# Attention score products on two row tiles of TensorE, one plain with one shifted head at a time

## What is computed

```
def _mha(q_in, k_in, v_in, Wq, Wk, Wv, bv, causal):
    q, k, v = projections of q_in, k_in, v_in to 16 heads of 16 values
    scores = einsum('bhse,bhte->bhst', q, k) * 16 ** -0.5
    if causal: scores = where(tril, scores, -inf)
    return softmax(scores) @ v, heads side by side
sa = _mha(x, x, x, ..., causal=True);   x = _layernorm(sa + x)
ca = _mha(x, ctx, ctx, ..., causal=False);   x = _layernorm(x + ca)
ffn = relu(x @ Wf1 + bf1) @ Wf2 + bf2;  x = _layernorm(x + ffn)
```

## Time and profile before

| | us |
|---|---|
| median of 3 runs (lowest, highest) | 1575.48 (1568.61, 1591.3) |
| the profiled execution, whole / its span | 1561.23 / 1559.5 |
| mean granted TensorE clock in it | 0.854 of 2.4 GHz |
| PE busy in the span | 1208.1 (77%) |
| DVE / ACT / POOL busy | 988.3 / 614.3 / 456.5 |
| PE plain products L403 (512) | 98.5 busy |
| PE shifted products L425 (512) | 76.6 busy |
| ACT exponentials L510 (128) | 117.2 busy |

### The profile page before, as it was taken

The page is one execution under the profiler, slowest core; times in us unless marked ns, Lnnn a source line. Parts: engine busy times, 40 slices in busy tenths (PEclk is TensorE's granted clock), DMA queues, the critical chain, the costliest instruction groups (busy, mean ns, idle before and its releaser), DMA issues. The chain is left out here.

```text
span 1559.5 us, 25872 instructions
## 1 busy us (share of the span) xinstructions
PE 1208.1 (77%) x9362; PEld 803.9 (52%) x9362; DVE 988.3 (63%) x2640; ACT 614.3 (39%) x1214; POOL 456.5 (29%) x609
## 2 busy tenths in 40 slices
PE   2898889999499710788888888830599996799998
PEld 1475555555278610577767677730254553345554
DVE  6646776676247530788888888845465651477776
ACT  1435556565255200566656665510054543000000
POOL 2325663323426644123333333245110100100000
PEclk9768998998689855799999999975586875699999
DMA  6313233221023234566566655335221211101000
GB/s 203 79 46 90 79 78 111 62 69 35 21 83 116 93 120 170 203 233 232 197 220 229 233 200 210 108 105 190 66 60 45 79 33 36 40 28 35 28 7 14
DMA packets 122052, 167.14 MB, mean 107 GB/s; under 512 B 13747, under 2 KB 96454, under 8 KB 118982
## 3 DMA queue, kind: packets, MB, share of 16 engines
q1 hardware_dynamic: 115894, 154.45, 30.1%
q0 software_dynamic: 3584, 8.92, 1.8%
q10 hardware_dynamic: 2448, 2.13, 0.4%
HBM read 123.31 MB, written 41.94 MB: 106 GB/s over the span
## 5 line engine op out<-in xcount | busy, mean ns | idle before, releaser
L1944 PE MATMUL moe_ps_u<-moe_x_hl,moe_up_hl 128*128 128x256 f16 x1932 | 226.8, 276 | 70.5 <-DVE moe_up_hl L2020 43.9
L1944 PEld LDWEIGHTS moe_ps_u<-moe_x_hl,moe_up_hl 128*128 128x128 f16 x1932 | 184.6, 99 | 112.7 <-DVE moe_up_hl L2020 50.4
L2307 PE MATMUL mix_ps_e<-wr_hl,mix_u_hl 128*128 128x512 f16 x768 | 173.4, 382 | 0.0
L2020 DVE SCALAR_TENSOR_TENSOR moe_up_hl<-moe_up_in,moe_up_hl 128x512 f16<-128x512 f32 x161 | 123.3, 798 | 55.5 <-ACT moe_up_hl L1993 55.5
L2064 POOL CAST moe_mid_hl<-moe_mid 128x256 f16<-128x256 f32 x161 | 71.7, 445 | 293.7 <-DVE moe_mid L2035 293.7
L2419 DVE SCALAR_TENSOR_TENSOR mix_acc<-mix_ps_e,mix_shares,mix_acc 128x256 f32<-128x256 f32 x256 | 110.3, 476 | 40.0 <-PE mix_ps_e L2307 39.7
L510 ACT ACTIVATE dec_probs<-dec_ps_t 128x768 f32<-128x768 f32 (+1 forms) x128 | 117.2, 917 | 38.5 <-PE dec_ps_t L425 38.1
L1993 ACT ACTIVATE moe_up_hl<-moe_up_in 128x512 f16<-128x512 f32 x161 | 99.2, 619 | 63.1 <-DMA moe_up_in<-in_moe_w 63.1
L1266 DVE TENSOR_REDUCE memory_neg_m<-memory_ps_s 128x2 f32<-128x512 f32 x128 | 84.8, 689 | 61.2 <-PE memory_ps_s L1043 58.6
L2307 PEld LDWEIGHTS mix_ps_e<-wr_hl,mix_u_hl 128*128 128x128 f16 x768 | 75.1, 98 | 84.0 <-issue 2.2
L403 PE MATMUL dec_ps_s<-dec_k_st,dec_q_st 48*128 48x256 f16 (+1 forms) x512 | 98.5, 277 | 20.3 <-DVE dec_neg_m L618 10.8
(11 more groups left out here) (278 smaller groups left out, 2098.0 us busy)
## 6 DMA issues: line engine op xcount, KB each, us to landing
moe_up_in<-in_moe_w SPq DMA_DIRECT2D x23, 1792.0 KB, 7.5
moe_down_in<-in_moe_w SPq DMA_DIRECT2D x23, 896.0 KB, 4.6
moe_raw<-in_mix_wr SPq DMA_DIRECT2D x32, 256.0 KB, 7.7
dec_q_st<-dec_q_dram SPq DMA_DIRECT2D x96, 64.0 KB, 2.7
dec_k_st<-dec_k_dram SPq DMA_DIRECT2D x96, 64.0 KB, 2.8
xs<-zeros SPq DMA_DIRECT2D x8, 736.0 KB
moe_x_in<-xs SPq DMA_DIRECT2D x23, 256.0 KB, 4.3
ys<-moe_y SPq DMA_DIRECT2D x23, 256.0 KB, 7.6
```

The costliest lines, as they stand in the source:

```text
L1944: mm = nc.tensor.matmul(bank[:, m, :], up_hl[t.slot][:, w, m, dc, f * P:(f + 1) * P], x_hl[t.slot][:, x, dc, :], start=(dc == 0 and w == x ...
L2020: nc.vector.scalar_tensor_tensor(up_hl[t.slot][:, LO, :, :, at].rearrange("p m c h -> p (m c) h"), up_in[t.slot][:, :, :, at].rearrange("p ...
L2307: mm = nc.tensor.matmul(ps_e[fill % RING][:, :, :], u_hl[t.slot][:, r, dc, k * P:(k + 1) * P], wr_hl[:, m, dc, 2 * q:2 * q + 2, :], start= ...
```

## The change

Even heads' stacks go to partitions 0-48 of `q_st` and `k_st`, odd heads' to 64-112, and each product names its row tile (`tile_position` row 0 or 64). `both_scores(t, p, j)` takes the place of `scores` and `shifted_scores`: it issues by turns the two plain matmuls of head 2p+j of item t+1 and the two shifted ones of head 2p+1-j of item t, one on each row tile. It is called with j=0 at a round's start and with j=1 where the round's second plain product stood, and `t_filled` is given by the second call. ACT's order of instructions in the steps is the same as before; so is DVE's. The heads are laid out so that the stacks are loaded by four transfers of 48 partitions for each half, from a DRAM copy that holds three parts (three stores for q, three for k, the high ones as soon as the high part is there). `load_m` is two transfers. The memsets move from DVE to POOL, all but two of the context's loads from ACT's start to places between SP's transfers (two go ahead of them).

```diff
+        def column(h):
+            return h // HALF * HALF + h % 2 * HALF // 2 + h % HALF // 2
...
-        q_st, k_st = ring(sb, "q_st", [64, HEADS, SEQ], F16), ring(sb, "k_st", [64, HEADS, SEQ], F16)
+        q_st, k_st = ring(sb, "q_st", [P, PAIRS, SEQ], F16), ring(sb, "k_st", [P, PAIRS, SEQ], F16)
...
-        q_dram, k_dram = dram("q_dram", [ITEMS, 2, D, SEQ], F16), dram("k_dram", [ITEMS, 2, D, SEQ], F16)
+        q_dram, k_dram = dram("q_dram", [ITEMS, 3, D, SEQ], F16), dram("k_dram", [ITEMS, 3, D, SEQ], F16)
+        Q_ROWS, K_ROWS = (HI, LO, HI), (HI, HI, LO)
...
-        STACK_DMAS, PARAMS = 6, 3 * LAYERS
+        STACK_DMAS, STORE_DMAS, ONES, PARAMS = 4, 3, 4, 3 * LAYERS
...
+                def load_context(b):
+                    sp.dma_start(ctx_raw[:, :, b * SEQ:(b + 1) * SEQ], ctx_src[b]).then_inc(ctx_loaded[b], 16)
+
+                for b in range(2):
+                    load_context(b)
+
+                def store(new, hl, kind, to, parts, stored):
+                    for part, ready, count in ((HI, hi_done, highs[kind, new]), (LO, near_emptied, near[kind, new] + 1)):
+                        sp.wait_ge(ready, count)
+                        for row in range(3):
+                            if parts[row] == part:
+                                sp.dma_start(to[new, row].rearrange("(c p) s -> p c s", p=P), hl[new % 2][:, part, :, :]).then_inc(stored[new % 2], 16)
 
                 def load_stacks(n, half):
                     if n >= 2:
                         sp.wait_ge(t_filled, PAIRS * (n - 2) + PAIRS // 2 * (half + 1))
                     else:
-                        sp.wait_ge(ones_set, 4)
-                    for frm, stored, to, parts in ((q_dram, q_stored, q_st, (0, 1, 0)), (k_dram, k_stored, k_st, (0, 0, 1))):
-                        sp.wait_ge(stored[n % 2], 16 * (n // 2 + 1))
-                        for row, part in enumerate(parts):
-                            sp.dma_start(to[n % 2][row * HD:(row + 1) * HD, half * HALF:(half + 1) * HALF, :],
-                                         frm[n, part].rearrange("(h e) s -> e h s", e=HD)[:, half * HALF:(half + 1) * HALF, :]
-                                         ).then_inc(stack_loaded[half][n % 2], 16)
+                        sp.wait_ge(ones_set, ONES)
+                    for frm, stored, to in ((q_dram, q_stored, q_st), (k_dram, k_stored, k_st)):
+                        sp.wait_ge(stored[n % 2], 16 * STORE_DMAS * (n // 2 + 1))
+                        stacks = frm[n].rearrange("l (e h) s -> (l e) h s", h=HEADS)
+                        for j in range(2):
+                            sp.dma_start(to[n % 2][64 * j:64 * j + STACK, half * HALF // 2:(half + 1) * HALF // 2, :],
+                                         stacks[:, half * HALF + j:(half + 1) * HALF:2, :]).then_inc(stack_loaded[half][n % 2], 16)
 
                 def load_m(n, half):
                     sp.wait_ge(far_emptied, far[TOP, half, n] + 1)
-                    sp.dma_start(q_st[n % 2][STACK:ROWS, half * HALF:(half + 1) * HALF, :],
-                                 m_row[half][n % 2][:, :]).then_inc(m_loaded[half][n % 2], 16)
+                    for j in range(2):
+                        sp.dma_start(q_st[n % 2][64 * j + STACK:64 * j + ROWS, half * HALF // 2:(half + 1) * HALF // 2, :],
+                                     m_row[half][n % 2][j * HALF // 2:(j + 1) * HALF // 2, :]).then_inc(m_loaded[half][n % 2], 16)
...
-                        store(new, q_hl, QUERY, q_dram, q_stored)
-                        store(new, k_hl, KEY, k_dram, k_stored)
+                        store(new, q_hl, QUERY, q_dram, Q_ROWS, q_stored)
+                        store(new, k_hl, KEY, k_dram, K_ROWS, k_stored)
                     if within(nxt):
                         load_m(nxt, 0)
                     if within(new):
                         load_stacks(new, 0)
+                    if t < 0:
+                        for b in range(3):
+                            load_context(3 * t + 8 + b)
+                    if t == -1:
+                        sp.dma_start(w_kv[:, :, :], wkv.rearrange("(c p) f -> p c f", p=P)).then_inc(w_kv_loaded, 16)
...
-                def scores(n, h):
-                    if h % HALF == 0:
-                        pe.wait_ge(stack_loaded[h // HALF][n % 2], 16 * STACK_DMAS * (n // 2 + 1))
-                    if HEADS * n + h >= 2:
-                        pe.wait_ge(max_done, HEADS * n + h - 1)
-                    for k in range(TT):
-                        mm = nc.tensor.matmul(ps_s[h % 2][:, k, 0:keys_of(n, k)], q_st[n % 2][0:STACK, h, k * P:(k + 1) * P],
-                                              k_st[n % 2][0:STACK, h, 0:keys_of(n, k)], start=True, stop=True)
-                    mm.then_inc(s_filled, 1)
...
-                def shifted_scores(n, p):
-                    if p % (PAIRS // 2) == 0:
-                        pe.wait_ge(m_loaded[2 * p // PAIRS][n % 2], 16 * (n // 2 + 1))
-                    if PAIRS * n + p >= 2:
-                        pe.wait_ge(exps_done, PAIRS * n + p - 1)
-                    for j in range(2):
-                        h = 2 * p + j
-                        for k in range(TT):
-                            a, b = queries_of(n, k)
-                            at = at_of(n, k)
-                            mm = nc.tensor.matmul(ps_t[p % 2][:, j, at:at + b - a], k_st[n % 2][0:ROWS, h, k * P:(k + 1) * P],
-                                                  q_st[n % 2][0:ROWS, h, a:b], start=True, stop=True)
-                    mm.then_inc(t_filled, 1)
+                def scores_ready(n, h):
+                    if h % HALF < 2:
+                        pe.wait_ge(stack_loaded[h // HALF][n % 2], 16 * STACK_DMAS * (n // 2 + 1))
+                    if HEADS * n + h >= 2:
+                        pe.wait_ge(max_done, HEADS * n + h - 1)
+
+                def scores(n, h, k):
+                    at, pair = 64 * (h % 2), h // 2
+                    return nc.tensor.matmul(ps_s[h % 2][:, k, 0:keys_of(n, k)], q_st[n % 2][at:at + STACK, pair, k * P:(k + 1) * P],
+                                            k_st[n % 2][at:at + STACK, pair, 0:keys_of(n, k)], start=True, stop=True, tile_position=(at, 0))
+
+                def shifted_ready(n, h):
+                    if h % HALF < 2:
+                        pe.wait_ge(m_loaded[h // HALF][n % 2], 32 * (n // 2 + 1))
+                    if PAIRS * n + h // 2 >= 2:
+                        pe.wait_ge(exps_done, PAIRS * n + h // 2 - 1)
+
+                def shifted_scores(n, h, k):
+                    row, pair = 64 * (h % 2), h // 2
+                    a, b = queries_of(n, k)
+                    at = at_of(n, k)
+                    return nc.tensor.matmul(ps_t[pair % 2][:, h % 2, at:at + b - a], k_st[n % 2][row:row + ROWS, pair, k * P:(k + 1) * P],
+                                            q_st[n % 2][row:row + ROWS, pair, a:b], start=True, stop=True, tile_position=(row, 0))
+
+                def both_scores(t, p, j):
+                    nxt, plain, other = t + 1, 2 * p + j, 2 * p + 1 - j
+                    if within(nxt):
+                        scores_ready(nxt, plain)
+                    if within(t):
+                        shifted_ready(t, other)
+                    for k in range(TT):
+                        if within(nxt):
+                            mm = scores(nxt, plain, k)
+                            if k == TT - 1:
+                                mm.then_inc(s_filled, 1)
+                        if within(t):
+                            mm = shifted_scores(t, other, k)
+                            if k == TT - 1 and j == 1:
+                                mm.then_inc(t_filled, 1)
...
-                pe.wait_ge(ones_set, 4)
+                pe.wait_ge(ones_set, ONES)
                 for t in STEPS:
                     nxt, new, old = t + 1, t + 2, t - 1
                     for p in range(PAIRS):
-                        if within(t):
-                            shifted_scores(t, p)
-                        if within(nxt):
-                            scores(nxt, 2 * p)
+                        both_scores(t, p, 0)
...
-                        if within(nxt):
-                            scores(nxt, 2 * p + 1)
+                        both_scores(t, p, 1)
...
-                for b in range(BATCHES):
-                    act.dma_start(ctx_raw[:, :, b * SEQ:(b + 1) * SEQ], ctx_src[b]).then_inc(ctx_loaded[b], 16)
-                act.dma_start(w_kv[:, :, :], wkv.rearrange("(c p) f -> p c f", p=P)).then_inc(w_kv_loaded, 16)
...
-                for k in range(2):
-                    nc.vector.memset(v[k][:, :, :, HD:VW], 0.0).then_inc(ones_set, 1)
-                dve.wait_ge(ones_set, 2)
-                for k in range(2):
-                    nc.vector.memset(v[k][:, :, :, HD:HD + 1], 1.0)
-                    nc.vector.memset(k_st[k][32:64, :, :], 1.0).then_inc(ones_set, 1)
...
```

(28 more changed lines are left out.)

## The result

The changed kernel takes 1644.17 us (median of four, 1634.28 to 1648.62) against 1573.96 before: a ratio of 1.0438, 95% interval 1.0392 to 1.0484. It is slower. The profiled execution has a span of 1632.5 us and a time of 1634.28, 73 us above the one read ahead of the prediction. Before's own median was 1557.5 in one of the later comparisons and 1574.2 in another, so kernels are compared here by their ratio to the kernel before on the same chip, and traces stretch by stretch.

The account below looks back on a forecast made before the run. PE was taken to bound cross steps nearly alone, causal ones by turns with DVE. Stalls +38, last step +3, clock +48, start -9 gave +80 on 1561.2: 1640 us, slower, range 1575 to 1690.

Parts of the forecast that it names:

- The bound, and the tiles: PE bounds cross steps nearly alone, causal ones by turns with DVE; overlapping row tiles make a both_scores call 0.24 us.
- The rival in which tiles don't overlap: Each both_scores call costs 0.44 us instead of 0.24, 33 us more at full clock: 1650 to 1690 us; chance 0.09.
- The stall and its place: Far pieces wait for ACT's copy behind the exponential: PE idle 1.25 us at five of eight cross-step borders, causal 1.10.
- The near chain: ACT's late copy of turned rows delays near pieces: PE idle 1.05 us before the query projection, 0.45 before the key's.
- the divide in round 7: DVE's divide, behind two maxima in round 7 of a cross step, costs PE 1.3 us.
- The cross step at full clock: 14.5 us of PE work plus 9.25 of waits: 23.8 us a step, +3.5 over before.
- The overlap wins: Rival: PE drops 45 us, the start 9, stalls mostly fall within today's waits: 1507 to 1535 us; chance 0.10.
- The causal step: 12.7 us of PE work plus 9.2 of waits: 21.9 us a step at full clock, +1.5 over before.
- The clock: Thinner PE work lowers the granted clock to 0.75 in the steps: 63 us, 15 lost today too, so +48.
- The start: Earlier DVE statistics and ACT high copy bring the first scores about 9 us sooner: -9, bounds 0 and 11.
- The rest: Step 15, with shifted products alone and the same borders, half of them under ACT's own work: +3 us.
- The rival of stalls without the clock: Stalls come in the steps but PE keeps 2.4 GHz: a little slower, 1578 to 1593 us; chance 0.18.

Follow-up runs that it names:

- the experiment on one tile: Changed kernel with each call pairing plain and shifted products of the same head, all four matmuls on one row tile: 1684.00 us, ratio 1.0823.
- the filled kernel: Changed kernel with PE repeating a shifted product four times ahead of the far piece in rounds 0, 1, 2, 4 and 5: 1614.57 us, ratio 1.0253.
- the first experiment: Changed kernel with only ACT's order altered, far copies and the near copies of rounds 0 and 1 ahead of the exponential: 1551.09 us, ratio 0.9935.

## Why the prediction was right, point by point

**The bound, and the tiles.** Right. Two calls, eight matmuls, take 0.46 (359.12 to the last start 359.46, and 0.12 for that one), so 0.23 each for 0.24 forecast, with both tiles starting on one time stamp. The rival in which tiles don't overlap falls by the timeline and by the experiment on one tile. The drain that the Trainium skill's page "TensorEngine Tiling (Array Packing)" (Key Properties) states for a change of tiling mode shows no price here: the values ahead of these calls take 1.01 us (358.11 to 359.12) for 1.00 before, and the calls their 0.23. Whether a value product and a call stand in different modes no row shows.

**The stall and its place.** Right: 1.25 forecast, 1.19 at the border shown. Over 15 steps the five borders a step would be 75 waits. 70 are for ACT's copies; behind seven of the causal items the border from round 7 to round 0 ends on POOL's `select` instead, which makes 77, two more than walked (the 1.9 us in 2 times of the list). The near chain (1.05 and 0.45 forecast) is 12.1 / 15 = 0.81 and 6.3 / 13 = 0.48, the divide in round 7 (1.3) 17.9 / 16 = 1.12. The cross step at full clock was put at 23.8; the filled kernel measures 24.35. For two thirds of the step its useless work isn't what makes the 0.5: from the turned outputs of round 2 to the values of round 0 it takes 16.43 us (340.99 to 357.42) and the changed kernel 16.55 (354.99 to 371.54). "The overlap wins" falls for the reason given against it, that the copy stands behind the exponential; the first experiment shows that this alone decides.

**The causal step.** The mechanism was right, the step somewhat too short. The last values' wait at the border from round 7 to round 0 was put at a stall of 1.10 and 0.4 more for POOL's `select`, 1.50 in all; it is 12.9 / 7 = 1.84, for the chain products, exponential, `select` starts a round's length later as well. PE timeline of the step from 197.50, its single such wait:

```profile
213.61 1.45 PE L476 MATMUL dec_ps_far<-dec_probs,dec_v 128*32 128x256 f32 x16 [1.97 <-POOL dec_probs L753]
```

What this step would be at full clock can be read from the filled kernel. PE runs at half clock behind that wait: from these values to the query projection it takes 5.43 us (213.61 to 219.04), and in the filled kernel 4.22 at full clock (211.58 to 215.80). So the 24.0 us are 22.8 at full clock, an estimate, for 21.9 forecast. Of these 0.9 a step, 6 us in all, 0.3 are the wait for `select`; the rest I can't place.

**The clock.** The direction was right and the size wrong, by the largest error of the sum. I took 0.75 for all steps; the seven causal steps together have 0.81 (0.63 to 0.93), the eight cross steps 0.82 (0.71 to 0.92). The prediction's own way of mixing both levels, with 0.81 (38% of the time at 1.2 GHz), gives 1 / (0.62 / 23.8 + 0.38 / 35) = 27.1 us for a cross step, against 27.4 measured. From the stretches: 185.2 - 11.4 - 7 x 22.8 = 14 and 211.1 - 8 x 23.8 = 21, together 35 us lost to half clock, for 63 forecast; less today's 15, **+20 for +48**. With 24.35 for the cross step at full clock, 4 of these us are stalls and the term is +16. The filled kernel's 29 us, as a least value of the gross amount, agree with either. I had taken the thin last steps (0.68) as the nearer neighbour; these steps lie nearer to the dense ones. The upper end of the term was also added up wrong: at 0.66 the same mixing gives some 91 us, not 85.

**The start.** Wrong: -9 forecast, +0.2 by the first mark. DVE's statistics did come early (6.47 for 13.90), but PE's first product started at 17.15 for 17.3, since `ones_set` is waited for at the head of PE's stream, and the memsets that give it had only moved to POOL. The line stands in the diff and I didn't follow it. The high copy came at 18.30 (20.04) and the first scores at 31.87 (35.72), and by the copy of step 0 these 3.9 us were gone again. The order of calls spent them: with the shifted pair first the first scores come at the same time (31.84), but the copy of step 0 at 55.45, 4.9 ahead of the kernel before. The walk had no stalls ahead of that copy. With PE's wait moved too, DVE is slow beside POOL's memsets instead, and the copy of step 0 stands at 60.55.

**The rest.** +8.1 for +3: 3.4 up to the feed-forward part, and 4.7 over the 1138 us behind it, in code that the change doesn't touch. In the profiled executions of all versions the same code takes 1113 to 1146 us, so 4.7 is within what it varies by; the cause is open.

**The sum.** Stalls 38 + 6, clock 20, start 0, rest 8: 72 of the 73 measured. The forecast's 80 was near in part by luck: a clock term 28 too large stood against three terms too small, the causal step by 6, the start by 9, the rest by 5. By the two ways of counting, stalls are 60 to 66% of the loss and clock 22 to 27%. The rival of stalls without the clock priced the stalls at 38 and gave 1578 to 1593; with the stalls at their measured size and the start at nothing it would still have missed the 16 to 20 us of the clock.

## What to carry to other kernels

Interleaving two kinds of work for a faster engine moves the moment at which each kind's last piece is done; look up who waits for that semaphore, and what stands behind that waiter in its queue, before you price the overlap. If a call can be split so that the piece others wait for still comes first (here the shifted pair on two tiles, 0.981 for 1.044), do that. Before work is moved from one engine to another to free the first, look for who waits for its signal: here the wait at the head of PE's stream kept PE's first product at 17.15 us (17.3 before), though DVE was ready 7.4 us sooner.

## What the runs showed of the hardware

- Matmuls of 48 and 49 rows on row tiles 0 and 64 carry the same start time (359.12, 359.24), and four of 256 columns take 0.23 us; on one tile they start 0.12 apart.
- Useless products made a kernel faster: 40 more matmuls a step (180 to 220 in the windows) took the granted clock from 0.81 to 0.93 and 1.00, and the ratio from 1.044 to 1.025. Lost overlap was paid twice here, once as a stall and once as clock; between the stalled and the unstalled order (the first experiment) the cross step goes from 27.40 at 0.81 to 20.08 at 1.00.
- Two `tensor_scalar` of 128x256 f32 on DVE took 5.40 us, for 0.74, beside memsets of 128x2048 f16 on POOL (1.8 us each). A memset moved off a busy engine wasn't free here while that engine worked.
